# A graph network kernel whose ring of gathered rows goes from twelve to fifteen slots

## The reference, cut to what matters

```python
def _L0_gnn_ref(x, edge_src, edge_dst, edge_w, w_self, w_neigh):      # pass 0, weighted sums
    msgs = edge_w[:, None] * x[edge_src]
    x_neigh = jax.ops.segment_sum(msgs, edge_dst, num_segments=N) @ w_neigh.T
    out = x @ w_self.T + x_neigh
    return out / jnp.maximum(norm, EPS)

def _gin_layer(h, src, dst, W1, b1, W2, b2, eps, gamma, beta):        # passes 1, 2, 3
    agg = jax.ops.segment_sum(h[src], dst, num_segments=N_NODES)
    z = (1.0 + eps) * h + agg
    m = jax.nn.relu(z @ W1 + b1) @ W2 + b2
    return jax.nn.relu(_layer_norm(m + h, gamma, beta))

# pass 4: graph convolution (segment_sum of scaled rows), then a top-2 mixture of 64 experts and a batch norm
# pass 5: e1 = segment_sum(edge_val[:, None] * x[edge_col], edge_row); out = (x - e1 * (diag + 1)) @ weight + bias
```

## Time and profile before

| | |
|---|---|
| median of the timed runs | 6352.02 us |
| profiled execution | 6397.59 us |
| its span, first to last instruction | 6395.8 us |
| TensorE busy | 5173.0 us, 81% |
| VectorE busy | 3873.3 us, 61% |
| GpSimd busy | 3694.9 us, 58% |
| ScalarE busy | 1677.2 us, 26% |
| granted TensorE clock, mean | 0.92 |
| gathered by the software queue | 624.43 MB of 1124.59 MB |

### The profile page before, as it was taken

The page is one execution under the profiler, slowest core; times in us unless marked ns, Lnnn a source line. Parts: engine busy times, 40 slices in busy tenths (PEclk is TensorE's granted clock), DMA queues, the critical chain, the costliest instruction groups (busy, mean ns, idle before and its releaser), DMA issues. The chain is left out here.

```text
span 6395.8 us, 104983 instructions
## 1 busy us (share of the span) xinstructions
PE 5173.0 (81%) x36139; PEld 4246.0 (66%) x36139; DVE 3873.3 (61%) x14138; ACT 1677.2 (26%) x4755; POOL 3694.9 (58%) x3731
## 2 busy tenths in 40 slices
PE   4888886688886888858888779888799955888887
PEld 3767764577775677746777667776688833777775
DVE  5777775367774777746777634445888635444444
ACT  2777774011110111111212200000233312333332
POOL 5565666566665666655666556666234352666665
PEclk8999998799998999989999889999899967899998
DMA  5444444666667666686666766666599942333333
GB/s 147 126 129 127 128 137 137 201 201 201 201 202 228 196 196 200 198 260 182 192 189 194 223 188 184 180 182 171 187 324 323 311 141 74 95 97 97 97 96 89
DMA packets 647058, 1124.59 MB, mean 176 GB/s; under 512 B 127578, under 2 KB 458456, under 8 KB 643804
## 3 DMA queue, kind: packets, MB, share of 16 engines
q0 software_dynamic: 211904, 624.43, 34.7%
q1 hardware_dynamic: 434618, 493.35, 24.1%
HBM read 990.13 MB, written 128.55 MB: 175 GB/s over the span
## 5 line engine op out<-in xcount | busy, mean ns | idle before, releaser
L2288 POOL DMA_INDIRECT ring<-planes,REC x1566 | 1511.3, 965 | 978.9 <-issue 417.3
L2385 PE MATMUL PS<-HH,pick 128*128 128x256 bf16 (+1 forms) x7836 | 1044.1, 278 | 193.7 <-issue 164.5
L2385 PEld LDWEIGHTS PS<-HH,pick 128*128 128x128 bf16 x7836 | 764.9, 99 | 384.2 <-issue 234.7
L2288 POOL DMA_INDIRECT ring<-in_x,REC x555 | 534.8, 964 | 338.4 <-PE PS L2364 157.0
L2288 POOL DMA_INDIRECT ring<-table,REC x498 | 478.3, 960 | 368.3 <-issue 242.0
L2288 POOL DMA_INDIRECT more<-planes,REC x522 | 503.4, 964 | 310.7 <-remote 145.1
L2361 PE MATMUL PS<-ring,pick 128*128 128x256 bf16 (+1 forms) x4698 | 640.9, 280 | 48.4 <-issue 43.5
L2385 PE MATMUL PS<-HH,ring 128*128 128x256 bf16 (+1 forms) x3924 | 551.1, 281 | 128.8 <-issue 96.9
L2364 PE MATMUL PS<-ring,pick 128*128 128x256 f32 x2106 | 582.0, 413 | 63.0 <-DMA ring<-table,REC 23.6
L2706 ACT ACTIVATE TZT<-PS 128x256 f32<-128x256 f32 (+1 forms) x294 | 133.7, 455 | 1662.1 <-remote 1084.7
L2361 PEld LDWEIGHTS PS<-ring,pick 128*128 128x128 bf16 x4698 | 467.3, 100 | 144.7 <-issue 67.7
(11 more groups left out here) (377 smaller groups left out, 9488.4 us busy)
## 6 DMA issues: line engine op xcount, KB each, us to landing
HH<-in_L_gnn_w SPq DMA_DIRECT2D x256, 512.0 KB
pick<-dense_blocks SPq DMA_DIRECT2D x480, 160.0 KB
ring<-dense_blocks SPq DMA_DIRECT2D x240, 160.0 KB
HH<-planes SPq DMA_DIRECT2D x64, 576.0 KB
dense_blocks<-HH SPq DMA_DIRECT2D x20, 1568.0 KB
planes<-pick SPq DMA_DIRECT2D x147, 192.0 KB
ring<-planes,REC POOLq DMA_INDIRECT x1566
table<-HN SPq DMA_DIRECT2D x147, 128.0 KB
```

Of the source, the lines that this page charges most:

```text
L2288: pool.indirect_dma_start(slot_row(k, slot, 0, RP if dense else D), None, planes[k] if dense else tables[k], bass.IndirectOffsetOnAxis(ap= ...
L2385: last = mm(bank(5 + n % 2, w), block, plane(m, t, w), start=t == 0 and m == 0, stop=t == NT - 1 and m == 2, skip_group_check=True)
```

## The change

`MORE` goes from 3 to 6, so the ring has 15 slots in 5 groups, and the buffer `more` holds six rows and six picks. The room comes from the scratch (4096 bytes in place of 8192), from `CNT` (64 columns), from `OFF`, which goes with its clear, and from `STI`, which now lies in `HS`.

```diff
-MORE = 3
+MORE = 6
 RING = (SLOTS + MORE) // GC
...
-        CNT = sb("CNT", NR + 2)
-        OFF = sb("OFF", NR + 2)
+        CNT = sb("CNT", NE)
...
-        STI = sb("STI", NT, i32)
+        STI = HS[:, 0:NT].bitcast(i32)
...
-            v.memset(OFF[:, :], 0.0)
...
-    nc = bacc.Bacc("TRN2", target_bir_lowering=False, num_devices=1, dynamic_dma_scratch_size=8192)
+    nc = bacc.Bacc("TRN2", target_bir_lowering=False, num_devices=1, dynamic_dma_scratch_size=4096)
```

## The result

| | before | after |
|---|---|---|
| median of 14 runs each, same chip | 6340.84 us | 6360.01 us |
| ratio, 95% interval | | 1.0029, 1.0021 to 1.0038 |
| profiled execution | 6397.59 us | 6357.2 us |

I had forecast 25 us less; it takes 19 us more. The shares of an engine and the waits of a place can be compared, differences of 20 us in the whole can't.

The account below looks back on a forecast made before the run. TensorE, busy 81% of the span, was taken as the bound, gather waits costing it 72.3 us. Ring 25 + picks 5 - starts 5 - scratch 0 = 25 us gain, 6352 to 6327 us; range 6292 to 6362.

Parts of the forecast that it names:

- waits that only move: Rival: TensorE waits at the following step instead of at a gather; 0 to 8 us faster, 6348 us; chance 27%.
- block loads that come later: Rival: bunched gathers delay dense-block loads in passes 1 to 4; 20 us slower, 6372 us; chance 11%.
- The scratch: Term: gather descriptors get 4 KB of each partition instead of 8; six gathers in flight, so cost 0.
- my fourth rival: Half the scratch throttles GpSimd, gather interval grows beyond 1.25 us; at 1.65 us, 230 us slower, 6580 us; chance 4%.
- The ring: Term: gathers run one group further ahead; of 37.7 us TensorE gather waits, two thirds gained, 25 us.
- the second case: Rival that waits only move to TensorE's following step: 0 to 8 us faster, 6348 us; chance 27%.
- The lower bound, 0: Lower end of the ring term: TensorE may lose at the next transpose what it gains at a gather.
- The picks: Term: VectorE may build selection matrices a group further ahead; bounds 0 and 85 us, 5 us gain taken.
- More gathers at a start: Term: GpSimd issues 15 gathers instead of 12 at starts of passes 1 to 4; 5 us loss, bounds 0 and 6.6.
- case 3: Rival: block loads come later behind bunched gathers, idle time before dense-block products grows; 20 us slower, 6372 us; chance 11%.
- the 5 us of loss: Loss taken for three more gathers at each start of passes 1 to 4, taking DMA time from loads.

Follow-up runs that it names:

- with padding: Kernel before, scratch cut to 4096 or 2048 bytes, unused bytes behind it so no buffer moves; slower chips 1.0017 (4096) and 1.0019 (2048).
- the fourth series: Slower chip, against the kernel before (6410.12 us): unchanged 0.9997, scratch of 4096 bytes alone 1.0014, the same with padding 1.0017.
- the fifth series: Another slower chip, against the kernel before (6331.01 us): scratch 2048 and padding 1.0019, changed kernel with ring of four groups 1.0030, changed kernel 1.0049.
- the first series: Slower chip, against the kernel before (6331.09 us): scratch alone 1.0022; changed kernel with four groups 1.0022, gathers five/picks four 1.0027, gathers four/picks five 1.0017.

## Why the prediction was wrong, point by point

Two steps failed: the two thirds of the gather waits that I took as a gain, and the scratch that I took as nothing. Of the 44 us between forecast and measurement the first is the larger part, 25 us, and without the second the result would be about no change. The measured 6360 us lies inside the range on record, 6292 to 6362; that is luck, since its upper end was set for waits that only move and for block loads that come later, not for what happened.

*The scratch, "So I take 0".* This step failed, and as far as the runs show it decides the sign. On slower chips the smaller scratch alone gave 1.0022 and 1.0014, with padding 1.0017 and 1.0019: 9 us (0.0014 x 6410) to 14 us (0.0022 x 6331). With the other vectors moved as well and a ring of four it gave 1.0022 and 1.0030. The bounds that I should have kept for it had no upper end in the rows, since no row showed the scratch at another size; I derived a zero from a count of gathers in flight. That count was a little high too: the gather issued at 1161.05 landed at 1166.99, 1.46 us before the matmul that I took it to release, and the row puts that wait down to "issue". The Trainium skill (DMA: Bandwidth & Descriptors, "Terms" and "The descriptor swizzle"), from which I had estimated that 28 gathers fit into 4096 bytes, gives zero by the same reasoning; the estimate is mine and not the skill's. The measured ratios disagree with it on the slower chips, though gathers went out at the old pace; on the faster ones (1.0003, 1.0000, 1.0006, 1.0007) they agree.

*By which way it costs* is open. It is not the way of my fourth rival, a throttled GpSimd: the median gather takes 946 to 949 ns and the next one follows 0.30 us later, with either size. It is not where the buffers lie (1.0017 with padding). It doesn't grow when the scratch is halved once more (1.0019 with 2048 bytes), which speaks against a cost for each time round the scratch. And it is absent on the faster chips. Single traces differ by more than the effect (in the fourth series the profiled execution with scratch and padding took 6409.29 us and the one of the unchanged kernel 6423.32), so I can't name the place. Most of all it isn't shown that it is the scratch's own doing and not that of any edit; a kernel with the full scratch and another small edit, and a series of scratch sizes between 4096 and 8192 with padding, both on a slower chip, would tell.

*The ring, "I take two thirds, 25 us".* The first half of the mechanism was there: 19 to 31 us fewer waits for gathers (72.3 to 52.9; 81.7 to 51.1), nearly all of those in the bfloat16 passes and nothing of those at the two starts, for the reasons given. That the end of pass 0 would shrink by 12 us didn't come: 13.7 of its 19.0 us stay, and from the first gather of the program to the first of pass 1 it is 1164.1 us for 1167.7 before, but 1165.9 for 1162.0 in the fifth series with five groups in place of four. The step that failed is the one from there to the time: that two thirds of the waits are gained because they sit at the ends of passes. On this kind of chip it is between nothing and a small loss. What the prediction called the second case (27%) is what the ring alone does there: the gather waits go, and no time is gained by it (ring of four 1.0022 and gathers five 1.0027 in the first series; 1.0030 and 1.0049 in the fifth). The lower bound, 0, was the row to go by: GpSimd waited for room hundreds of times, and a consumer that gets its rows earlier only meets its other waits earlier. On a faster chip the ring has the sign that I forecast and less than half of the size: 10.6 us by the medians of the kernels before and after.

*The picks.* VectorE's waits at the picks of pass 4 fell from 114.9 us to 30.6 (in the main ring alone from 85.2 to 11.4), much more than I had thought, and it is the picks' own depth that does it. No time follows that can be told from none (gathers four and picks five groups: 1.0017; the other way about: 1.0027; the ring of four: 1.0022). The 5 us that I took, 0.0008 of the time, are below what these intervals resolve.

*More gathers at a start, and the block loads.* The idle time before the block products is unchanged to 0.3 us; case 3 is out, and the 5 us of loss don't show. I also read those rows wrongly: I called the 322.5 us waits for loads, and they say themselves that 164.5 + 96.9 of them have no releaser.

*The sum.* Forecast 25 + 5 - 5 - 0; measured on slower chips about 0 + 0 - 0 - 9 to 14 where one part was tried at a time, against 19 for the whole (1.0029). The rest of 5 to 10 us is within the intervals, or belongs to the depth: in the fifth series the ring of five stands 11 us above that of four by the medians, with intervals that overlap. The runs don't settle it.

## What to carry to other kernels

A change that pays for a buffer with another resource has two terms, and the payment deserves its own experiment: here the edit of one number, the scratch, told more than the trace could. Such an experiment needs a neutral edit beside it, on the same chip, and not only the unchanged kernel. Waits taken from an engine that has other waits close behind are worth only what the engine's total idle time falls by, so compare that total (span less busy) and not the waits that one aimed at, and over several traces, since the totals scatter too. And here, where the producer is 20% faster than its consumer, the deeper ring was worth about nothing; at 4%, as on the faster chips, it was worth 0.16%.

## What was unexpected in the hardware

The same program takes 5635 to 5638 us on two chips and 6331 to 6410 on two others. Each series ran on one chip at one time, and one chip went from 6331 to 6410 us between two series, so what belongs to the chip and what to the moment can't be told apart. On a slower chip TensorE is busy 246 us longer in the unchanged kernel, and idle 537 us longer (1237.3 against 700.8), while VectorE (3874.7 and 3869.5 us) and GpSimd (3698.9 and 3700.9) work as long as on a faster one. Part of that stands before the block products, without a releaser. The page of the unchanged kernel on the slower chip, and TensorE's timeline in pass 3 there:

```profile
span 6421.7 us, 104983 instructions
PE 5184.4 (81%) x36139; PEld 4255.7 (66%) x36139; DVE 3874.7 (60%) x14138; ACT 1676.5 (26%) x4755; POOL 3698.9 (58%) x3731
...
L2385 PE MATMUL PS<-HH,pick 128*128 128x256 bf16 (+1 forms) x7836 | 1061.1, 281 | 188.3 <-issue 157.7
L2385 PE MATMUL PS<-HH,ring 128*128 128x256 bf16 (+1 forms) x3924 | 548.5, 281 | 119.6 <-issue 87.9
```

```profile
3031.97 0.27 PE L2385 MATMUL PS<-HH,ring 128*128 128x256 bf16 x1 [0.45 <-issue]
3032.67 0.27 PE L2385 MATMUL PS<-HH,ring 128*128 128x256 bf16 x1 [0.43 <-issue]
3033.38 0.49 PE L2385 MATMUL PS<-HH,ring 128*128 128x256 bf16 x3 [0.44 <-issue]
```

The idle time before the block products is 307.9 us here and 111.7 on the faster chip. The matmuls come one by one, some 0.7 us apart, with 0.4 us of idle time that nothing in the profile released. Counted over the whole trace, 683 idle times of 0.1 to 1 us before a matmul have no releaser, 297 us together; on the faster chip there are 30, 13 us together. The granted clock is 0.917 there and 0.943 on the faster chip. What holds the matmuls no run here shows. The gaps also mean that the 322 us before the block products, which I had read as waits for loads, are on this kind of chip for the most part something else: 245.6 of the 307.9 us here are put down to no releaser.
